# Turning y by way of a DRAM scratch and VectorE, with the products of k and v at other places

## The reference

```
x = x + tanh(g_xattn) * xattn(values=ctx, keys=ctx, query=layernorm(x), mask, Wv, bv, Wk, bk, Wq, bq, Wo, bo)
x = x + tanh(g_ffn)   * tanh(((layernorm(x) @ W1) @ W2) @ W3 + b_ffn)
xattn: softmax(where(mask == 0, min, q k^T) / sqrt(16)) v, per head, then @ Wo + bo
```

## Time and profile before

| | |
|---|---|
| median of 3 runs | 1095.0 us (1094.87 to 1095.42) |
| the profiled execution's own time | 1093.47 us |
| its span, first to last instruction | 1091.3 us |
| PE / PEld busy | 1043.5 / 913.9 us |
| DVE / ACT / POOL busy | 907.2 / 823.4 / 773.7 us |
| DMA | 127.92 MB, 16 engines 40.1% busy in the main queue |

### The profile page before, as it was taken

The page is one execution under the profiler, slowest core; times in us unless marked ns, Lnnn a source line. Parts: engine busy times, 40 slices in busy tenths (PEclk is TensorE's granted clock), DMA queues, the critical chain, the costliest instruction groups (busy, mean ns, idle before and its releaser), DMA issues.

```text
span 1091.3 us, 45222 instructions
## 1 busy us (share of the span) xinstructions
PE 1043.5 (96%) x18723; PEld 913.9 (84%) x18723; DVE 907.2 (83%) x1272; ACT 823.4 (75%) x1275; POOL 773.7 (71%) x1184
## 2 busy tenths in 40 slices
PE   5988999999999999999999999999999999999965
PEld 4777888888888888888888888888888888888855
DVE  5778888888888888888888888888888888888766
ACT  4566887787787787778778778777877877877742
POOL 5255787787777778778777777877877777777653
PEclk9999999999999999999999999999999999999987
...
GB/s 162 44 95 123 102 110 139 114 112 134 133 106 122 142 107 113 141 114 114 132 119 120 121 143 109 110 141 114 114 132 132 105 123 136 110 115 113 85 121 69
DMA packets 180158, 127.92 MB, mean 117 GB/s; under 512 B 109809, under 2 KB 146930, under 8 KB 179954
## 3 DMA queue, kind: packets, MB, share of 16 engines
q1 hardware_dynamic: 179810, 124.77, 40.1%
...
...
HBM read 70.46 MB, written 53.48 MB: 114 GB/s over the span
## 4 chain that ended last, share of the span: by engine, by line
PE 90%; DVE 5%; SPq 2%; issue 2%; DMA 2%; ACT 0%; DVEq 0%
PE ps_m L475 17%; PE ps_m L468 17%; PE ps_s L568 13%; PE ps_s L589 13%; PE ps_x L600 11%; PE ps_m L530 9%; PE ps_m L462 6%; PE ps_s L574 4%; DVE neg_max L949 2%; DVE probs L960 2%; DMA a_rows<-scratch_a 0%; DMA den<-a_den 0%; DMA scratch_m<-max_T 0%; SPq L204 0%; PE ps_m L613 0%
## 5 line engine op out<-in xcount | busy, mean ns | idle before, releaser
L949 DVE TENSOR_REDUCE neg_max<-ps_s 128x16 f32<-128x2048 f32 x128 | 293.2, 2291 | 81.0 <-PE ps_s L574 81.0
L960 DVE TENSOR_TENSOR probs<-ps_s,far_T 128x2048 f32<-128x2048 f32 x128 | 293.3, 2291 | 15.5 <-PE ps_s L589 9.7
L760 ACT ACTIVATE probs<-probs 128x2048 f32<-128x2048 f32 x128 | 244.5, 1910 | 8.2 <-DVE probs L960 7.9
L735 ACT ACTIVATE q_aug<-ps_m,q_bias,q_scale 128x256 f32<-128x256 f32 x256 | 123.4, 563 | 159.3 <-PE ps_m L468 150.8
L409 POOL TENSOR_TENSOR y<-y,th 128x512 f32<-128x512 f32 x58 | 73.9, 1275 | 160.7 <-ACT th L781 122.2
L568 PE MATMUL ps_s<-k_aug,q_aug 32*128 32x128 f32 x4096 | 150.7, 283 | 16.7 <-DVE probs L960 8.2
L568 PEld LDWEIGHTS ps_s<-k_aug,q_aug 32*128 32x128 f32 x4096 | 128.1, 186 | 39.2 <-issue 31.3
L589 PE MATMUL ps_s<-q_aug,k_aug 32*128 32x128 f32 x4096 | 151.4, 283 | 4.1 <-DVE neg_max L949 2.3
L589 PEld LDWEIGHTS ps_s<-q_aug,k_aug 32*128 32x128 f32 x4096 | 127.1, 186 | 21.8 <-issue 4.2
L600 PE MATMUL ps_x<-probs,v_ones 128*32 128x128 f32 x4096 | 139.8, 278 | 4.1 <-issue 2.8
L600 PEld LDWEIGHTS ps_x<-probs,v_ones 128*32 128x32 f32 x4096 | 105.2, 110 | 33.2 <-issue 33.2
(11 more groups left out here) (120 smaller groups left out, 1720.3 us busy)
## 6 DMA issues: line engine op xcount, KB each, us to landing
...
ctx_in<-in_ctx SPq DMA_DIRECT2D x252, 64.0 KB, 3.4
q_aug<-scratch_m SPq DMA_DIRECT2D x256, 4.0 KB
scratch_m<-max_T SPq DMA_DIRECT2D x128, 16.0 KB
```

The source lines that it names most:

```text
L735: last = nc.scalar.activation(dst[:, :, 2 * m + a, :], src[:, m * TOK:(m + 1) * TOK].rearrange("p (n q) -> p n q", q=P), ACT.Identity, bia ...
L760: nc.scalar.activation(tile, tile, ACT.Exp).then_inc(probs_ready, 1)
L949: nc.vector.tensor_reduce(neg_max[:, 0:H].rearrange("p (j c) -> p j c", j=G), ps_s[:], AX.X, ALU.max, negate=True).then_inc(max_ready, 1)
L960: nc.vector.tensor_tensor(probs[i % 2][:].rearrange("p j s q -> p (j s) q"), ps_s[:].rearrange("p j s q -> p (j s) q"), far_T[:].unsqueeze ...
```

## The change

For pairs 0 to 58 (`END`) y is turned otherwise. `normalise_y` (POOL) writes yn as before. SP then writes yn to a DRAM scratch (`write_y`, at the end of turn t for pair t-4), and in the next turn reads it back in four DMAs of 32 x 64 blocks (`read_y`, behind the loads of ctx). VectorE turns the blocks in one instruction (`turn_y`, ahead of the second maxima) into y_T in SBUF, which ACT and VectorE split into yT as before. TensorE's `turn_y` is left for the last five pairs. Since blocks interleave even and odd columns, W1 W2 W3 is multiplied with its rows interleaved likewise.

From pair 5 on (`Q_EARLY`) k's product stands in the odd half turn where `turn_y` and nine of v's twelve matmuls stood, v's first seven matmuls stand behind q's in the even half, and its last five in the odd half. q moves to bank 0. `turn_x` goes ahead of f. On SP `read_den` goes behind `write_max(2t)`. On POOL and ACT some steps are ordered anew (`low_of_a` ahead of the normalisation, `high_of_a` and `keep_v` earlier, `high_of_x` ahead of `high_of_ctx`); on VectorE both halves of x's statistics stand ahead of the first maxima.

```diff
...
 scratch_r = nc.dram_tensor("scratch_r", [2 * G, KT * TOK], F32, kind="Internal").ap()
+scratch_y = nc.dram_tensor("scratch_y", [PAIR, P, E], F32, kind="Internal").ap()
 scratch_m = nc.dram_tensor("scratch_m", [2, 2 * H, P], F32, kind="Internal").ap()
...
-BANK = {"cT": 1, "xT": 0, "k": 0, "q": 1, "v": 1, "yT": 2, "o": 2, "f": 2}
+Q_EARLY = 5
+
+BANK = {"cT": 1, "xT": 0, "k": 0, "q": 0, "v": 1, "yT": 2, "o": 2, "f": 2}
...
         return ps_m[2]
+    if p < Q_EARLY and name == "q":
+        return ps_m[1]
     if p == 0 and name == "v":
...
+    def write_y(p):
+        sp.wait_ge(yn_ready, PAIR * (p + 1))
+        wait(sp, y_blocks_landed, 16 * G * p)
+        sp.dma_start(scratch_y.rearrange("n s e -> s n e"), yn[:]).then_inc(yn_stored, 16)
+
+    def read_y(p):
+        sp.wait_ge(yn_stored, 16 * (p + 1))
+        wait(sp, y_turned, p)
+        for a in range(G):
+            sp.dma_start(y_blocks[a * 32:(a + 1) * 32].rearrange("c n (b e) -> c (n b) e", e=64),
+                         scratch_y[:, :, a * 64:(a + 1) * 64].rearrange("n (b c) e -> c (n b) e", c=32)
+                         ).then_inc(y_blocks_landed, 16)
+
     def store(p):
...
             load_ctx(t + 3)
+        if is_pair(t - 5):
+            read_y(t - 5)
+        write_max(2 * t)
         if is_pair(t - 2):
             read_den(t - 2)
-        write_max(2 * t)
-        if is_pair(t - 2):
             write_a(t - 2)
...
             read_wide(t - 2)
+        if is_pair(t - 4) and t - 4 <= END:
+            write_y(t - 4)
     y3, y2, y1, last = NP - 4, NP - 3, NP - 2, NP - 1
...
     def normalise_y(p):
-        wait(pool, yT_done, p)
+        if p <= END + 1:
+            wait(pool, yn_stored, 16 * p)
+        else:
+            pool.wait_ge(yT_done, p - 1 - END)
         pool.wait_ge(y_ready, p + 1)
...
     def turn_y(p):
-        if p < NP - 5:
-            pe.wait_ge(y_ready, p + 2)
-        else:
-            pe.wait_ge(k_ready, NP)
-            wait(pe, yT_ready, p if p < NP - 1 else 0)
+        pe.wait_ge(k_ready, NP)
+        wait(pe, yT_ready, p if p < NP - 1 else 0)
         pe.wait_ge(yn_ready, PAIR * (p + 1))
-        transposes(bank("yT", p), yn_of(p)).then_inc(yT_done, 1)
+        for k in range(KT):
+            for b in range(PAIR):
+                last = nc.tensor.transpose(bank("yT", p)[:, k * TOK + b * P:k * TOK + (b + 1) * P],
+                                           yn_of(p)[:, b, k::KT], ident[:])
+        last.then_inc(yT_done, 1)
...
             pe.wait_ge(xT_ready, p + 1)
+        if p >= Q_EARLY:
+            pe.wait_ge(q_ready, p + 1)
         pe.wait_ge(cT_ready, p + 1)
...
             pe.wait_ge(q_ready, 1)
-        if p > 1:
+        if 1 < p < Q_EARLY:
             pe.wait_ge(v_ready, p)
...
             pe.wait_ge(cT_ready, 1)
-        if p > 0:
+        if 0 < p < Q_EARLY:
             pe.wait_ge(q_ready, p + 1)
+        if p >= Q_EARLY:
+            pe.wait_ge(v_ready, p)
+            pe.wait_ge(cT_ready, p + 1)
         dst = bank("v", p)
         products = [(i, n) for i in range(PAIR) for n in range(len(TERMS))]
-        for i, n in products[:9] if part == 0 else products[9:]:
+        first = 9 if p < Q_EARLY else 7
+        for i, n in products[:first] if part == 0 else products[first:]:
             k, a, b = TERMS[n]
...
             pe.wait_ge(product_kept, 1)
-            multiply(wT_s, w3_s)
+            multiply(wT_s, w3_s, [slice(m * P, (m + 1) * P) for m in range(KT)])
         if stage == 2:
...
             pe.wait_ge(product_kept, 3)
-            multiply(wT_s, w23_s)
+            multiply(wT_s, w23_s, [slice(m, E, KT) for m in range(KT)])
         if stage == 4:
...
                     make_o(t - 4)
-                if t < 4:
-
+                if t + 1 < Q_EARLY:
                     make_q(t + 1)
             else:
-                if is_pair(t - 5):
-                    turn_y(t - 5)
                 if t == NP - 1:
                     weigh_values(i - 2)
-                if is_pair(t + 1):
+                if t + 1 < Q_EARLY:
                     make_v(t + 1, 0)
+                elif is_pair(t + 1):
+                    make_k(t + 1)
             if is_batch(i - 1):
...
             if half == 0:
-                if t >= 4 and is_pair(t + 1):
+                if t + 1 < Q_EARLY:
+                    make_k(t + 1)
+                elif is_pair(t + 1):
                     make_q(t + 1)
-                if is_pair(t + 1):
-                    make_k(t + 1)
+                    make_v(t + 1, 0)
             else:
...
                     make_v(t + 1, 1)
+                if is_pair(t + 2):
+                    turn_x(t + 2)
                 if is_pair(t - 5):
                     make_f(t - 5)
-                if is_pair(t + 2):
-                    turn_x(t + 2)
             product(i)
...
         wait(act, f_done, p if p < NP - 1 else 0)
-        high(yT_of(p), bank("yT", p)[:], yT_done, p + 1, yT_high)
+        if p <= END:
+            high(yT, flat(y_T[:]), y_turned, p + 1, yT_high)
+        else:
+            high(yT_of(p), bank("yT", p)[:], yT_done, p - END, yT_high)
...
             gate(t - 6)
+        if t >= Q_EARLY:
+            keep_v(t)
+        if is_pair(t - 3):
+            high_of_a(t - 3)
         if is_pair(t + 1):
...
             exponents(2 * t - 1)
-        if is_pair(t + 1):
+        if t + 1 < Q_EARLY:
             spread_k(t + 1)
-        if is_pair(t - 5):
-            high_of_y(t - 5)
         if is_batch(2 * t - 2):
...
             keep_a(2 * t - 1)
-        if is_pair(t - 3):
-            high_of_a(t - 3)
-        if is_pair(t + 1):
+        if is_pair(t - 5):
+            high_of_y(t - 5)
+        if t + 1 >= Q_EARLY and is_pair(t + 1):
+            spread_k(t + 1)
+        if t + 1 < Q_EARLY:
             keep_v(t + 1)
         if is_pair(t + 2):
+            high_of_x(t + 2)
             high_of_ctx(t + 2)
...
             keep_f(t - 5)
-        if is_pair(t + 2):
-            high_of_x(t + 2)
         if t == 2:
...
     def low_of_y(p):
-        low(yT_of(p), bank("yT", p)[:], yT_high, p + 1, yT_ready)
+        low(yT_of(p), flat(y_T[:]) if p <= END else bank("yT", p)[:], yT_high, p + 1, yT_ready)
+
+    def turn_y(p):
+        dve.wait_ge(y_blocks_landed, 16 * G * (p + 1))
+        wait(dve, yT_ready, p)
+        nc.vector.transpose(y_T[:].rearrange("p k (g c) -> p g k c", c=32),
+                            y_blocks[:].rearrange("p n (b r k) -> p (n b) k r", k=KT, r=32)).then_inc(y_turned, 1)
...
             stats_of_x(t + 3, 0)
+            stats_of_x(t + 3, 1)
+        if t > 0 and is_pair(t + 2):
+            moments_of_x(t + 2)
         if is_batch(2 * t):
...
             moments_of_y(t - 4)
-        if t > 0 and is_pair(t + 2):
-            moments_of_x(t + 2)
+        if is_pair(t - 5):
+            turn_y(t - 5)
         if is_batch(2 * t + 1):
             maxima(2 * t + 1)
-        if is_pair(t + 3):
-            stats_of_x(t + 3, 1)
-        turn_max(2 * t + 1)
         if is_pair(t - 2):
             reciprocals(t - 2)
+        turn_max(2 * t + 1)
         if is_pair(t - 5):
...
         if t == 3:
```

13 lines of the change are left out of this document (8 added, 5 removed).

## The result

| | before | after |
|---|---|---|
| median on the same chip | 1095.21 us (1094.87 to 1095.8) | 1154.07 us (1152.83 to 1159.39) |
| profiled execution, its span | 1093.47, 1091.3 us | 1153.29, 1151.5 us |

The changed kernel is slower: ratio 1.0546, 95% interval 1.0512 to 1.058. The direction is as forecast, the size isn't: +59 us where +18 was forecast, outside the range of 1067 to 1150 us.

What follows compares the result with a forecast made beforehand. The prediction took PE's work to bound the kernel and SP's queue to be late next: 56 turns at 16.4 instead of 16.06 us, +19, last three -1.4, total +17.6 us; median forecast 1113 us, range 1067 to 1150.

Steps and rivals of the forecast that it cites:

- The ring of ps_s: Waits on the single tile ps_s, scores to scores_T to next scores: 7.76 us a batch, 15.52 us a turn at least.
- w: Start of write_max(2t+1) in SP's queue, from which queue times are counted; forecast 12.09 us into its turn.
- Part 1: PE loses the four transposes of y: a turn of 15.6 us if nothing else is late, 0.45 us gained.
- Part 2: DVE turns y's blocks in 0.70 us, at no cost while the blocks are there in time.
- Part 3: Five DMAs of y in SP's queue make the even maxima late: a turn of 16.4 us.
- L: Time from w until the even batch's maxima are in q_aug: 17.0 us forecast against 14.4 before.
- d: Delay of scores_T of the even batch, which lengthens the odd half: 0.9 us forecast, the turn being 15.52 + d.
- has four to spare: POOL is busy for 12.1 us of a turn, so yn was taken to be in time for write_y.
- y's blocks hold up VectorE: Rival: late blocks delay turn_y and the second maxima; turn 17.0 us, 1146 us, chance 0.15.
- The write lands as quickly as the page's rule says: Rival: write_y has landed by w + 6.4; turn 15.9 us, 1086 us, chance 0.10.
- SP's queue has room: Rival: the queue's spare of 1.4 us is enough if write_y lands soon; turn 15.6 us, 1068 us, chance 0.20.
- The gain goes into the bank: Rival: SP in time, turn_x 0.25 us late at the bank of k and x; 15.85 us, 1083 us, chance 0.05.

Runs made afterwards that it cites:

- e5: Changed kernel without write_y and read_y (VectorE turns a constant tile), turn_x back behind f, x's statistics and high_of_x in their old places: 1085.42 us, 0.9898.
- e20: e18 with xn ahead of yn on POOL: 1092.01 us, 0.9957.
- e6: Changed kernel with y turned by PE again and no DMAs of y, all other moves kept: 1121.33 us, 1.0241.
- e10: Changed kernel with turn_x behind f, x's statistics and high_of_x as before the change, y's DMAs kept: 1146.7 us, 1.045.
- e14: Changed kernel with write_y ahead of read_max(2t+1) and read_wide in SP's queue: 1150.02 us, 1.0467.
- e15: e14 plus yn ahead of xn on POOL, turn_x behind f, read_y ahead of ctx, even maxima ahead of write_a, ctx and x: 1117.75 us, 1.018.
- e18: e15 with low_of_a back behind xn on POOL: 1099.36 us, 1.0007.
- e19: Changed kernel with yn ahead of xn and low_of_a behind both on POOL: 1154.95 us, 1.0518.
- e11: e10 with VectorE's turn_y behind turn_max(2t+1): 1151.79 us, 1.0493.
- e3: Changed kernel with VectorE's turn_y moved from ahead of the second maxima to behind turn_max(2t+1): 1172.14 us, 1.0695.
- e12: Changed kernel with SP's order write_max(2t), read_y, read_max(2t), then read_den, write_a, load_x: 1130.72 us, 1.0284.
- e4: Changed kernel with the four reads of y issued in ACT's queue ahead of spread_q, write_y kept on SP: 1267.36 us, 1.1534.

## Why the prediction was right in direction and wrong in size

- **What bounds before, and what would be late next: right.** The path by SP's queue, which had 2% of the chain, is the one that got late, at the place forecast and for the DMA forecast.
- **The ring of ps_s, 7.76 us a half: right**, 7.78 in the even halves. w lies 12.08 us into the turn, 12.09 forecast.
- **Part 1, PE's turn of 15.6 us: right as a floor, wrong for this order.** e5 and e20 reach 15.69 and 15.62; the changed kernel never gets below 15.97, since `turn_x` waits for the bank of k. This was priced at 0 to 0.25 us and measures 0.38, by e6's waits 0.37 us a turn. While scores_T is late most of it is hidden, as the prediction said (e10 gets 10 us back).
- **Part 2, VectorE's transpose at 0.70 us: right** (0.69), and rarely in anyone's way: it waited for its blocks in 17 of 59 turns, 14.7 us in all.
- **Part 3, the queue: the right path, L too short.** In means over the turns, from w: `write_y` at 3.99 (3.80 forecast), its landing in 4.8 (4.9), `read_y` at 8.84 (8.7), `write_max(2t+2)` at 11.2 (10.9), `write_a` at 13.2 (12.8), and scores_T follows at 17.7. So L is about 17.6, not 17.0: 0.4 us of it is there by `write_a`, the rest comes behind it. By the forecast's own d = (L - 15.2)/2 that is a turn of 16.7 us; the median is 16.81.
- **The landing of the write.** The 2.6 us worked out from the Trainium skill ("DMA: Bandwidth & Descriptors", the anatomy of one DMA) is not what these rows show: 4.7 us in the median, as the like store suggested. The page gives its formula for DMAs that GpSimd issues, and this one is issued by SP. In e14 the same write takes 2.7 us. What the two differ by is how long before it SP issued the last 256 KB read: the list at the end lays five kernels side by side.
- **The step that failed: L = 17.0 us, taken for every turn and with PE at full clock.** As a size, L is 0.6 us short; the median turn is 16.81 us instead of 16.4. As one value for all turns it leaves out what long waits bring: in seven of the eight turns of 18 us or more the granted clock falls, and those seven lose 12 us behind scores_T. The sum had no term for the clock. That is nearly all of the 13 us by which the mean turn is above the median. The sum over 56 turns: forecast +19; the median turn, +23; the mean is 17.04, another +13. Together 55 us. Measured from scores to scores, turns 6 to 60 lose 53 us, and turn 6 starts 6.7 us later than before, where the forecast had 0.3: turn 0 is 2.7 us longer, and turn 5, the first in the new order, takes 19.35 us. What makes these two long wasn't looked into.
- **What doesn't explain the long turns.** The landing of the write spreads from 4.0 to 7.1 us, but five of the eight long turns have a landing of 4.4 to 5.1, and e14, where none is above 4.3, has four. What makes one wait of PE end in a fall of the clock and another not isn't shown either: waits of 1.7 and 1.8 us did, waits of 2.0 and 2.8 us didn't.
- **A term that was missing, and is hidden here: POOL's order.** The prediction wrote that POOL is busy for 12 of 16 us and "has four to spare". For yn that held in the changed kernel, where SP never waits for it. But the time isn't to spare: in e15 POOL idles 3.3 us a turn ahead of `divide_a`, and all that follows, to xn, is one chain. The moves of `finish` and `low_of_a` got no price and no cover. Once the maxima are in time `low_of_a` is worth 19 us (e15 to e18) and xn ahead of yn 5 (e18 to e20). `finish` was never moved by itself. In e6 they cost next to nothing: PE waits for xn twice. In the changed kernel `low_of_a` is hidden behind SP's queue (e19); in e15, where 40 of the 60 us are back, it is most of what is left.
- **The rivals.** "y's blocks hold up VectorE" named 1146 us, nearest to the measured time, and isn't the main mechanism: VectorE waits for blocks in 17 of 59 turns only, and taking them out of the maxima's way changed nothing clear of noise (e11 against e10) or cost more (e3). It bounds once the maxima are sent first (e12) or the reads stand in ACT's queue (e4). "The write lands as quickly as the page's rule says" (the Trainium skill's) and "SP's queue has room" are refuted by the 4.7 us and the 48 waits. "The gain goes into the bank" is real, but mostly hidden (e10).

Open are the landings of the write above 5.5 us, what decides whether the clock falls behind a wait, and what keeps e20's mean turn 0.35 us above its shortest.
